# VectorE adds the scattered window sums to the node table from PSUM, with the mask as a per-partition scalar

## The chip, the cores and the metric

One core of one Trainium2 chip. The metric is the device time of one execution in microseconds, the median of several.

## The reference

Two layers of an equivariant graph network over 12,500 nodes and 200,000 edges, sorted by destination. Each layer gathers the source node's 32 features for every edge, computes from an MLP of the edge (64 hidden, 256 or 384 weights) the weights that mix them, and adds the resulting 32-wide message to the destination node. Around each layer stands a residual addition and a normalisation over the features.

```python
    edge_index = jnp.stack([src, dst])
    x = _layernorm(x + _L0_gnn_ref(x, edge_index, edge_attr_4, edge_attr_32, ...), axis=-1)
    x = _layernorm(x + _L1_gnn_ref(x, edge_weight, edge_attr_3, edge_index, ...), axis=-1)
```

In layer 0: `h = relu(edge_feat @ W1 + b1)`, `w = (h @ W2 + b2).reshape(e, 4, 8, 8)`, products of `w` with the gathered scalars and vectors and the edge's harmonics, and `segment_sum` over `dst`. Layer 1 has the same shape, with the distance as the MLP's input and seven paths.

## The kernel before

The edges are cut into 98 chunks of 2048 (16 tiles of 128). Each layer runs a loop over the chunks with two slots (z = 0, 1) for every buffer; the five engines each run their own program, ordered by semaphores alone. A prologue starts the first chunk, and a tail ends the last.

GpSimd gathers the source rows: 16 indirect DMAs per chunk, one per tile (`gather`, L340). It may run ahead by the two slots of `rows`.

TensorE computes the edge weights from the hidden values into PSUM (`weigh`, L624: 4 halves in layer 0, 8 in layer 1), adds up part of the products by a multiplication with the identity (`sum_products`, L637), and scatters the messages (`scatter`, L651): for each of 4 groups of 4 tiles it multiplies a one-hot matrix, made by ScalarE from the destination index modulo 128, with the messages cut into three bf16 parts, into `acc` (128 x 32 per group, in PSUM).

VectorE multiplies weights from PSUM with the gathered values (L899 and L906 in layer 0, L913 in layer 1; `multiply`), sums the rest of the products (L924), finishes the messages (L1022, L1026, L1029; L1072, L1078, L1086, L1095), cuts them (L932, L938), prepares the next chunk's rows (L948, L962, L974, L976; L952, L966, L983), and adds the previous chunk's windows to the node table (L990).

The window: the destinations of a group lie within 128 successive nodes, so they touch two neighbouring blocks of the table (2 x 32 columns). Which partition belongs to which block is said by two masks of 0 and 1 per group, kept in `plan` (16 columns of negative keys, then 4 x 2 masks). ScalarE's `split_windows` (L488) makes two masked copies of each group's `acc` in SBUF (`split`, 4 x 64 columns), 8 activations per chunk; VectorE's `add_window` (L990) adds 64 columns of `split` to the table at an address loaded into a register. The four windows of a chunk are added one after the other, because they may overlap; each waits for the one before. Other VectorE work stands between them.

In layer 0 the order in `body0` is: L948, window 0, window 1, L974, L976, window 2, L962, L1022, L1026, window 3, L1029, then the multiplications with the cuts L932 and L938 between them, and L924 twice. In layer 1 (`body1`): multiplications 0 to 5 between the message steps, L938, window 0, L966, window 1, L924, window 2, the seventh multiplication (L913), window 3, the eighth, L983, L924.

ScalarE: copies the chunk's plan (L450), computes the distances to an iota (L460), the one-hots (L469), the hidden values (L404, L406, L411), row copies (L434, L437, L438, L445), the copy of the sums (L478) and the masked copies (L488).

Of the kernel before, what the change touches and what calls it, by code (L numbers as in the profile page):

```python
# [9 lines left out]
ALU = mybir.AluOpType  # L10
# [68 lines left out]
BODY_STEPS, PROLOGUE_STEPS, TAIL_STEPS = (9, 10), (6, 7), (10, 12)  # L79


def build(nc, x, x_nodes, x_self, src, dst, dst_rows, sh, feat, rel, dist, identity, w1_0, b1_0, w2_0, si, w1_1, b1_1,
# [6 lines left out]
    with ExitStack() as ctx:  # L89
# [55 lines left out]
        plan_sb = slots(lambda z: sb(f"slot_plan{z}", [P, PLAN]))  # L145
# [4 lines left out]
        split = slots(lambda z: sb(f"split{z}", [P, GROUPS, 2 * FEAT]))  # L150
# [40 lines left out]
        class LayerSemaphores:  # L191


            def __init__(self, n):
# [28 lines left out]
                self.windows_split = ring("windows_split")  # L223
# [148 lines left out]
        def _(act):  # L372
# [90 lines left out]
            def one_hots(n, z, steps):  # L463

                s = layers[n]
                for half in range(2):
# [26 lines left out]
            def loop(n, count):  # L493
                s = layers[n]

                def body(i, z, r, last, steps):
# [10 lines left out]
                    if not tail:  # L507
                        distances(n, z1, r1, 1, steps)
                        if n == 0:
                            one_hots(n, z1, steps)  # L510
# [4 lines left out]
                    if n == 1:  # L515
                        if not tail:
                            one_hots(n, z1, steps)
                        if not last:
                            copy_rows(n, i + 1, z, r + 1)
                    if n == 0:  # L520
                        split_windows(n, z, r)
                        if not last:
                            hide(n, z, r + 1, 1)
# [4 lines left out]
                    if n == 1:  # L528
                        split_windows(n, z, r)

                with act.Fori(0, count) as j:
# [15 lines left out]
                    one_hots(n, 0, steps)  # L547
# [36 lines left out]
        def _(pe):  # L584
# [56 lines left out]
            def scatter(n, z, r):  # L641
# [4 lines left out]
                pe.wait_ge(s.windows_split[z], r)  # L646
# [644 lines left out]
```

## Time and profile before

| | us |
|---|---|
| runs | 4531.0, 4531.57, 4543.85 |
| median | 4531.57 |
| the profiled execution | 4544.37 |
| its span | 4542.6 |
| mean granted TensorE clock over the span | 0.922 of 2.4 GHz |

| engine | busy us | share |
|---|---|---|
| TensorE matmul | 3766.9 | 83% |
| VectorE | 3963.2 | 87% |
| ScalarE | 2346.9 | 52% |
| GpSimd | 3167.3 | 70% |

Layer 0 lies in about the first half of the span, layer 1 in the second. Times in the rows are from the start of the span; PE is TensorE, DVE VectorE, ACT ScalarE, POOL GpSimd. An instruction's row gives its duration; successive instructions of one engine overlap by a little, so that the next can start before the one in front has ended.

### The profile page before, as it was taken

What the parts mean: (1) busy time and instruction counts of PE and PEld (TensorE: products, weight loads), DVE (VectorE), ACT (ScalarE), POOL (GpSimd) and SP (SyncE); (2) the same over time, 40 slices, a digit from 0 to 9 for tenths busy, and PEclk for the clock granted to TensorE, in tenths of its full rate; (3) what the DMA queues carried; (4) which work ended last, traced back from release to release, by engine and by line L of the source; (5) the groups of instructions that cost most, each with busy time, mean ns of one, the idle gap of its engine ahead of it and who ended that gap; (6) DMA issues with size and microseconds to landing.
All of it is one profiled execution on the core that took longest, in us unless ns stands there. A gap on an engine that the chain in (4) does not pass through costs nothing.

```text
span 4542.6 us, 66084 instructions
## 1 busy us (share of the span) xinstructions
PE 3766.9 (83%) x19258; PEld 2237.4 (49%) x19258; DVE 3963.2 (87%) x4658; ACT 2346.9 (52%) x6473; POOL 3167.3 (70%) x3145
## 2 busy tenths in 40 slices
PE   5887887888787878887189999999999999999995
PEld 3555555555555555555034444444444444444442
DVE  6878788787887788877889999999999999999998
ACT  2555555555555555555045555555555555555553
POOL 6777777777777777777266667766766777667661
PEclk7998898888888988888589999999999999999997
DMA  2111111111111111111322121212121212121221
GB/s 91 28 23 28 28 23 28 28 23 28 27 25 28 23 28 28 23 28 23 76 49 43 34 43 34 43 34 44 34 43 34 43 34 43 34 43 37 40 40 21
DMA packets 206517, 159.45 MB, mean 35 GB/s; under 512 B 123073, under 2 KB 186562, under 8 KB 199234
## 3 DMA queue, kind: packets, MB, share of 16 engines
q1 hardware_dynamic: 76978, 89.79, 8.4%
q0 software_dynamic: 100352, 51.58, 7.9%
q10 hardware_dynamic: 29170, 17.88, 1.4%
q8 instruction: 7, 0.11, 0.0%
q14 instruction: 10, 0.08, 0.0%
HBM read 148.58 MB, written 10.43 MB: 35 GB/s over the span
## 4 chain that ended last, share of the span: by engine, by line
POOL 35%; PE 31%; issue 22%; DVE 10%; DVEq 1%; POOLq 0%; DMA 0%; ACT 0%; SPq 0%; ACTq 0%
POOL rows L340 35%; PE wps L624 16%; PE red L637 15%; DVE prod L913 6%; DVE t_b L1086 1%; DVE sums L924 0%; DVE q L983 0%; DVE t_b L842 0%; DVE work L823 0%; DVEq L897 0%; POOLq L357 0%; DVEq L1151 0%; DVE work L1195 0%; DVE table L1193 0%; DVE node_a L1196 0%
## 5 line engine op out<-in xcount | busy, mean ns | idle before, releaser
L624 PE MATMUL wps<-w_sb,hidden 128*128 128x256 f32 (+1 forms) x6272 | 2185.5, 506 | 669.6 <-DVE prod L906 394.8
L340 POOL DMA_INDIRECT rows<-x_rows,src x1568 | 1544.1, 985 | 755.7 <-issue 468.5
L624 PEld LDWEIGHTS wps<-w_sb,hidden 128*128 128x128 f32 x6272 | 1305.1, 213 | 1489.4 <-issue 518.5
L340 POOL DMA_INDIRECT rows<-in_x,src x1568 | 1615.2, 1030 | 506.3 <-issue 499.4
L637 PE MATMUL red<-prod,ident 128*128 128x384 f32 (+1 forms) x3136 | 1200.5, 536 | 0.0
L924 DVE TENSOR_REDUCE sums<-prod 128x192 f32<-128x1536 f32 (+2 forms) x392 | 1099.2, 2823 | 0.0
L460 ACT ACTIVATE gap<-iota,slot_plan 128x128 bf16<-128x128 f32 x3136 | 956.6, 387 | 264.1 <-DVE t_b L1086 179.4
L913 DVE TENSOR_TENSOR prod<-wps,q 128x896 f32<-128x896 f32 x784 | 844.8, 1086 | 96.3 <-PE wps L624 95.4
L637 PEld LDWEIGHTS red<-prod,ident 128*128 128x128 f32 x3136 | 594.8, 190 | 584.3 <-issue 396.5
L488 ACT ACTIVATE split<-acc,slot_plan 128x32 f32<-128x32 f32 x1568 | 300.1, 302 | 664.6 <-PE acc L651 635.2
L899 DVE TENSOR_TENSOR prod<-wps,q 128x768 f32<-128x768 f32 x392 | 374.0, 954 | 126.6 <-PE wps L624 126.2
L469 ACT ACTIVATE onehot<-gap 128x1024 bf16<-128x1024 bf16 x392 | 389.5, 1041 | 0.0
L906 DVE TENSOR_TENSOR prod<-wps,q 128x768 f32<-128x768 f32 x392 | 372.3, 950 | 0.0
L404 ACT ACTIVATE hidden<-hps,b_sb 64x512 f32<-64x512 f32 x196 | 134.9, 688 | 414.7 <-PE hps L603 414.7
L478 ACT ACTIVATE sums<-red 128x384 f32<-128x384 f32 (+1 forms) x196 | 105.9, 540 | 467.0 <-PE red L637 467.0
L948 DVE TENSOR_TENSOR t_a<-rows,geo 128x384 f32<-128x384 f32 x98 | 55.3, 564 | 289.3 <-DMA rows<-in_x,src 289.3
L651 PEld LDWEIGHTS acc<-msg,onehot 128*128 128x128 bf16 x3136 | 243.3, 96 | 81.9 <-issue 81.9
L651 PE MATMUL acc<-msg,onehot 128*128 128x32 bf16 x3136 | 255.8, 176 | 16.5 <-issue 15.4
L411 ACT ACTIVATE hidden<-mlp,b_sb,w1c_sb 64x1024 f32<-64x1024 f32 x196 | 231.0, 1226 | 72.2 <-issue 72.2
L651 PEld LDWEIGHTS acc<-rest,onehot 128*128 128x128 bf16 x3136 | 240.0, 96 | 43.1 <-issue 42.4
L651 PE MATMUL acc<-rest,onehot 128*128 128x32 bf16 x3136 | 255.3, 176 | 0.0
L651 PE MATMUL acc<-last_part,onehot 128*128 128x32 bf16 x3136 | 255.2, 176 | 0.0
(112 smaller groups left out, 2372.6 us busy)
## 6 DMA issues: line engine op xcount, KB each, us to landing
mlp<-in_dist SPq DMA_DIRECT2D x98, 512.0 KB, 5.0
mlp<-in_feat SPq DMA_DIRECT2D x98, 256.0 KB, 2.9
rows<-in_x,src POOLq DMA_INDIRECT x1568, 2.4
rows<-x_rows,src POOLq DMA_INDIRECT x1568
frames<-prod ACTq DMA_DIRECT2D x4, 1764.0 KB, 5.9
geo<-frames ACTq DMA_DIRECT2D x98, 72.0 KB, 1.9
src<-in_src SPq DMA_DIRECT2D x196, 8.0 KB, 1.6
geo<-in_sh ACTq DMA_DIRECT2D x98, 32.0 KB, 1.8
```

The lines of the kernel that those rows point to most:

```text
L340: nc.gpsimd.indirect_dma_start(out=rows[z][:, t, :], out_offset=None, in_=table_rows, in_offset=bass.IndirectOffsetOnAxis(ap=src_sb[z][:, ...
L411: nc.scalar.activation(hidden[0:HID, z, c0:c0 + 2 * SET], mlp_sb[z][0:HID, c0:c0 + 2 * SET], ACT.Relu, bias=b1_sb[0:HID, 1:2], scale=w1c_s ...
L460: ins = nc.scalar.activation(gap[:, t, :], iota[:], ACT.Abs, bias=plan_sb[z][:, t:t + 1])
L469: ins = nc.scalar.activation(onehot[z][:, t0:t1, :], gap[:, t0:t1, :], ACT.Relu, scale=-1.0, bias=1.0)
L488: ins = nc.scalar.activation(split[z][:, g, w * FEAT:(w + 1) * FEAT], acc[z][:, g * FEAT:(g + 1) * FEAT], ACT.Identity, scale=plan_sb[z][: ...
L624: ins = nc.tensor.matmul(wps[:, col:col + W_PATHS[n] * MM], hidden[:, z, e0:e0 + P], w2, start=True, stop=True)
L637: ins = nc.tensor.matmul(red[:, 0:cols], ident[:], pr[:, i, :, a:b, :], start=(i == 0), stop=(i == MUL - 1))
L651: ins = nc.tensor.matmul(acc[z][:, g * FEAT:(g + 1) * FEAT], onehot[z][:, t, :], cut[part][:, t, :], start=(tg == 0 and part == 0), stop=( ...
L899: nc.vector.tensor_tensor(pr[:, :, 1, t0:t0 + T, :].rearrange("p i t (m o) -> p t m i o", m=3), w[:, :, 3 * MM:4 * MM].rearrange("p t (i o ...
L906: ins = nc.vector.tensor_tensor(pr[:, :, 0, t0:t0 + T, :].rearrange("p i t (a o) -> p t a i o", a=3), w[:, :, 0:3 * MM].rearrange("p t (a ...
L913: ins = nc.vector.tensor_tensor(pr[:, :, 0, t0:t0 + T, :].rearrange("p i t (a o) -> p t a i o", a=7), w[:, :, 0:C].rearrange("p t (a i o) ...
L924: st.done(nc.vector.tensor_reduce(sums_by_half(n)[:, :, t0:t1, :], products(n)[:, :, :, t0:t1, :].rearrange("p i h t c -> p h t c i"), AX_ ...
```

## The change

`split` and `split_windows` go. VectorE's `add_window` reads `acc` in PSUM itself: for each group two scalar_tensor_tensor instructions of 32 columns, table = acc x mask + table, with the mask column as the per-partition scalar. The masks get a buffer of their own, `mask_sb`, apart from the keys in `plan_sb`, filled by a new ScalarE copy at the end of each body (`copy_masks`), which waits until VectorE has added the windows that used that slot before (`windows_added`) and signals `masks_copied`. `add_window` for the first group waits for `scattered` and `masks_copied`; after the last group it waits for its own last instruction and increments `windows_added`, for which TensorE's `scatter` waits in place of `windows_split`. ScalarE's `copy_plan` now waits for the one-hots of the slot, and `one_hots` for the scatter that read them. The first addition, which in the kernel before added a zeroed `split`, now reads a zeroed `acc` with zeroed masks. (In the prologue two steps are counted in place of one.)

```diff
-BODY_STEPS, PROLOGUE_STEPS, TAIL_STEPS = (9, 10), (6, 7), (10, 12)
+BODY_STEPS, PROLOGUE_STEPS, TAIL_STEPS = (9, 10), (7, 8), (10, 12)
...
-                act.wait_ge(layers[n].windows_split[z], r)
-                steps.done(nc.scalar.activation(plan_sb[z][:], plan[:, bass.ds(k, 1), :].rearrange("p k c -> p (k c)"),
-                                                ACT.Copy))
+                act.wait_ge(layers[n].onehot_ready[z], r)
+                steps.done(nc.scalar.activation(plan_sb[z][:], plan[:, bass.ds(k, 1), 0:TILES].rearrange(
+                    "p k c -> p (k c)"), ACT.Copy))
+
+            def copy_masks(n, k, z, r):
+
+                act.wait_ge(layers[n].windows_added[z], r)
+                nc.scalar.activation(mask_sb[z][:], plan[:, bass.ds(k, 1), TILES:PLAN].rearrange("p k c -> p (k c)"),
+                                     ACT.Copy).then_inc(layers[n].masks_copied[z], 1)
...
+                act.wait_ge(s.scattered[z], r)
...
-            def split_windows(n, z, r):
-
-                s = layers[n]
-                act.wait_ge(s.scattered[z], r + 1)
-                for g in range(GROUPS):
-                    for w in range(2):
-                        ins = nc.scalar.activation(split[z][:, g, w * FEAT:(w + 1) * FEAT],
-                                                   acc[z][:, g * FEAT:(g + 1) * FEAT], ACT.Identity,
-                                                   scale=plan_sb[z][:, TILES + g * 2 + w:TILES + g * 2 + w + 1])
-                ins.then_inc(s.windows_split[z], 1)
...
-                pe.wait_ge(s.windows_split[z], r)
+                pe.wait_ge(s.windows_added[z], r)
...
-            def add_window(g, cols, z, st):
-
+            def add_window(n, g, cols, z, r, st, final=False):
+
+                s = layers[n]
                 if g:
                     st.need(add_window.last)
+                else:
+                    dve.wait_ge(s.scattered[z], r)
+                    dve.wait_ge(s.masks_copied[z], r)
                 window = flat[:, bass.ds(cols[g], 2 * FEAT)]
-                add_window.last = st.done(nc.vector.tensor_tensor(window, window, split[z][:, g, :], ALU.add))
+                for w in range(2):
+                    part = window[:, w * FEAT:(w + 1) * FEAT]
+                    ins = nc.vector.scalar_tensor_tensor(
+                        out=part, in0=acc[z][:, g * FEAT:(g + 1) * FEAT],
+                        scalar=mask_sb[z][:, g * 2 + w:g * 2 + w + 1], in1=part, op0=ALU.mult, op1=ALU.add)
+                add_window.last = st.done(ins)
+                if g == GROUPS - 1 and not final:
+                    st.need(add_window.last)
+                    dve.sem_inc(s.windows_added[z], 1)
...
-                dve.wait_ge(s.windows_split[z1], r + z)
-                add_window(0, cols, z1, st)
-                add_window(1, cols, z1, st)
+                add_window(0, 0, cols, z1, r + z, st)
+                add_window(0, 1, cols, z1, r + z, st)
...
-                    st.need(st.done(nc.vector.memset(split[1][:], 0.0)))
+                    st.done(nc.vector.memset(mask_sb[1][:], 0.0))
+                    st.need(st.done(nc.vector.memset(acc[1][:, 0:GROUPS * FEAT], 0.0)))
```

In ScalarE's body the masked copies stood before the second half of the hidden values in layer 0 and at the end in layer 1; `copy_masks` stands at the end in both.

## Rows read from the trace of the kernel before

**Rows 1.** The page: busy time, share of the span and instructions of each engine.

```profile
PE 3766.9 (83%) x19258; PEld 2237.4 (49%) x19258; DVE 3963.2 (87%) x4658; ACT 2346.9 (52%) x6473; POOL 3167.3 (70%) x3145
```

**Rows 2.** Busy times by stretch: one chunk of layer 0, one of layer 1.

```profile
core 0: us, PE busy (x) PEld busy (x) DVE busy (x) ACT busy (x) POOL busy (x), PEclk, DMA share, GB/s
1005.93:1027.33 21.40, 16.84 (x100) 11.81 (x99) 17.26 (x23) 11.81 (x33) 16.46 (x16) 0.92 0.10 14
3297.43:3319.82 22.39, 20.52 (x97) 10.21 (x96) 21.69 (x24) 12.11 (x34) 16.07 (x18) 1.00 0.33 63
```

**Rows 3.** Timeline of GpSimd in layer 0: start us, duration us, instruction, idle before.

```profile
1003.51 0.94 POOL L340 DMA_INDIRECT rows<-in_x,src  x1 [0.30 <-issue]
1004.76 0.94 POOL L340 DMA_INDIRECT rows<-in_x,src  x1 [0.30 <-issue]
1006.01 1.30 POOL L340 DMA_INDIRECT rows<-in_x,src  x1 [0.30 <-issue]
1007.61 0.95 POOL L340 DMA_INDIRECT rows<-in_x,src  x1 [0.30 <-issue]
1008.87 1.64 POOL L340 DMA_INDIRECT rows<-in_x,src  x1 [0.30 <-issue]
1010.81 0.94 POOL L340 DMA_INDIRECT rows<-in_x,src  x1 [0.30 <-issue]
...
1013.31 1.25 POOL L340 DMA_INDIRECT rows<-in_x,src  x1 [0.30 <-issue]
```

**Rows 4.** Timeline of VectorE over the same stretch of layer 0.

```profile
1005.93 0.56 DVE L948 TENSOR_TENSOR t_a<-rows,geo 128x384 f32<-128x384 f32 x1 [3.62 <-DMA rows<-in_x,src]
1006.41 0.58 DVE L990 TENSOR_TENSOR table<-table,split 128x64 f32 x2
...
1007.10 0.67 DVE L976 TENSOR_TENSOR q<-rows,geo 128x384 f32<-128x384 f32 x1
...
1008.28 0.55 DVE L1022 TENSOR_TENSOR t_b<-sums,geo 128x384 f32<-128x384 f32 x1
1008.74 0.29 DVE L1026 TENSOR_TENSOR msg<-sums 128x128 f32<-128x128 f32 x1
1008.94 0.22 DVE L990 TENSOR_TENSOR table<-table,split 128x64 f32 x1
1009.08 0.60 DVE L1029 TENSOR_TENSOR msg<-t_b,sums 128x384 f32<-128x384 f32 x1
...
1010.46 0.95 DVE L906 TENSOR_TENSOR prod<-wps,q 128x768 f32<-128x768 f32 x1
...
1013.05 0.69 DVE L932 TENSOR_TENSOR rest<-msg 128x512 f32<-128x512 f32 x1
```

**Rows 5.** Costliest groups: busy us, mean ns of one, idle before. Layer 0's gathers.

```profile
L340 POOL DMA_INDIRECT rows<-in_x,src x1568 | 1615.2, 1030 | 506.3 <-issue 499.4
```

**Rows 6.** Timeline of VectorE in layer 1, around the four windows of a chunk.

```profile
3297.43 0.21 DVE L990 TENSOR_TENSOR table<-table,split 128x64 f32 x1
3297.57 1.34 DVE L966 TENSOR_REDUCE q<-t_a 128x384 f32<-128x1152 f32 x1
...
3301.35 0.21 DVE L990 TENSOR_TENSOR table<-table,split 128x64 f32 x1
3301.78 1.09 DVE L913 TENSOR_TENSOR prod<-wps,q 128x896 f32<-128x896 f32 x1 [0.22 <-PE wps L624]
3302.79 0.21 DVE L990 TENSOR_TENSOR table<-table,split 128x64 f32 x1
3303.29 1.09 DVE L913 TENSOR_TENSOR prod<-wps,q 128x896 f32<-128x896 f32 x1 [0.28 <-PE wps L624]
```

**Rows 7.** Timeline of TensorE in layer 1, ahead of the sums L637.

```profile
3314.10 1.77 PE L624 MATMUL wps<-w_sb,hidden 128*128 128x448 f32 x4 [0.51 <-DVE prod L913]
```

**Rows 8.** Costliest groups: ScalarE's masked copies and the old window addition.

```profile
L990 DVE TENSOR_TENSOR table<-table,split 128x64 f32 x792 | 172.3, 218 | 23.6 <-ACT split L488 4.8 <-issue 4.2
...
L488 ACT ACTIVATE split<-acc,slot_plan 128x32 f32<-128x32 f32 x1568 | 300.1, 302 | 664.6 <-PE acc L651 635.2
```

**Rows 9.** Groups of instructions by form: L773, in the set-up.

```profile
L773 DVE SCALAR_TENSOR_TENSOR table<-wps,table 128x512 f32<-128x512 f32 x6 | 3.9, 686 | 1.4 <-PE wps L592 1.4
L773 DVE SCALAR_TENSOR_TENSOR table<-wps,table 128x64 f32<-128x64 f32 x1 | 0.2, 216 | 0.0
```

More of the change, by code:

```diff
@@ L144, in build @@
         hidden = sb("hidden", [P, RING, CHUNK])
-        plan_sb = slots(lambda z: sb(f"slot_plan{z}", [P, PLAN]))
+        plan_sb = slots(lambda z: sb(f"slot_plan{z}", [P, TILES]))
+        mask_sb = slots(lambda z: sb(f"slot_masks{z}", [P, 2 * GROUPS]))
         gap = sb("gap", [P, TILES, P], BF16)
@@ L222, in __init__ @@
                 self.scattered = ring("scattered")
-                self.windows_split = ring("windows_split")
+                self.windows_added = slots(lambda z: sem(f"l{n}_windows_added{z}"))
+                self.per_chunk.append((self.windows_added[0], 1))
+                self.masks_copied = ring("masks_copied")
                 self.dve_body = sem(f"l{n}_dve_body")
@@ L461, in distances, with one_hots @@
                 steps.done(ins)
-            def one_hots(n, z, steps):
+            def one_hots(n, z, r, steps):
                 s = layers[n]
+                act.wait_ge(s.scattered[z], r)
                 for half in range(2):
@@ L509, in body @@
                         if n == 0:
-                            one_hots(n, z1, steps)
+                            one_hots(n, z1, r1, steps)
                     if not last:
@@ L516, in body @@
                         if not tail:
-                            one_hots(n, z1, steps)
+                            one_hots(n, z1, r1, steps)
                         if not last:
                             copy_rows(n, i + 1, z, r + 1)
[L520 to L523, printed above, removed]
+                    if n == 0 and not last:
+                        hide(n, z, r + 1, 1)
                     if n == 1 and not last:
@@ L527, in body @@
                         copy_sums(n, z1, r1)
-                    if n == 1:
-                        split_windows(n, z, r)
+                    copy_masks(n, k, z, r)
                 with act.Fori(0, count) as j:
@@ L546, in loop @@
                         distances(n, 0, r0, half, steps)
-                    one_hots(n, 0, steps)
+                    one_hots(n, 0, r0, steps)
                     if n == 1:
@@ L1026, in body0 @@
                 nc.vector.tensor_tensor(msg[z][:, :, 0:MUL], sm[:, :, 0, :], sm[:, :, 1, :], ALU.add)
[L1027 removed]
+                add_window(0, 3, cols, z1, r + z, st)
                 dve.wait_ge(s.geo_used[z], r + 1)
@@ L1103, in body1 @@
                 cols = load_columns(k)
-                dve.wait_ge(s.windows_split[z1], r + z)
-                add_window(0, cols, z1, st)
+                add_window(1, 0, cols, z1, r + z, st)
                 if not last:
@@ L1108, in body1 @@
                     project_sum(1, z)
-                add_window(1, cols, z1, st)
+                add_window(1, 1, cols, z1, r + z, st)
                 if not tail:
                     sum_tiles(1, z1, r1, 0, st)
-                add_window(2, cols, z1, st)
+                add_window(1, 2, cols, z1, r + z, st)
                 if not tail:
                     multiply(1, z1, r1, 6)
-                add_window(3, cols, z1, st)
+                add_window(1, 3, cols, z1, r + z, st)
                 if not tail:
```

7 lines of the change are left out of this document (2 added, 5 removed).

## The prediction

> **What bounds the kernel now.** I read the page's busy shares first. No engine is idle enough to be ruled out, since VectorE has 87%, TensorE 83% and GpSimd 70% [rows 1], but these are means over two layers with different limits, so I read each layer from one chunk of its own. In layer 0 a chunk takes 21.40 us, of which VectorE is busy for 17.26 us; in layer 1 it takes 22.39 us, of which VectorE is busy for 21.69 and TensorE for 20.52 [rows 2].
>
> Layer 0 is set by GpSimd. Its 16 gather instructions for a chunk follow each other without a break: undisturbed, one starts 1.25 us after the other, of which 0.94 us is the instruction [rows 3]. Sixteen times 1.25 is 20.0 us of the 21.4. VectorE stood idle for 3.62 us before it could start the body of this chunk, and what it waited for was the gathered rows [rows 4]. The missing 1.4 us are in the gathers that take longer: 1.30, 1.64 and 1.25 us in place of 0.94 [rows 3], together 1.37 us. Over the layer the mean is 1030 ns [rows 5], so with 0.945 for an undisturbed one 1568 x (1.030 - 0.945) = 133 us, or 1.36 us a chunk.
>
> What lengthens them is seen by laying GpSimd's rows on VectorE's. The gather at 1006.01 ends its extra 0.36 us when L948 is nearly through (1005.93 + 0.56 = 1006.49). The gather at 1008.87 starts inside an unbroken run L1022, L1026, L990, L1029, ending at 1009.68; its extra 0.70 us brings it to 1009.57. The gather at 1013.31 meets L932, ending at 1013.74, and gets 0.31 us, to 1013.62 [rows 3, 4]. In all three the gather is held until about 0.12 us before the end of the VectorE instruction that runs when it starts, or of the last in an unbroken run, and all these instructions read two tensors from SBUF. The gather at 1010.81, which starts in L906 with one input in PSUM and one in SBUF, takes 0.94 us. The one at 1007.61 starts 0.16 us before the end of L976 and takes 0.95 us though an L990 follows: a gather that finds a gap gets through [rows 3, 4].
>
> The Trainium skill says the same of the mechanism (GPSIMD Engine Reference, "Key points": GpSimd's SBUF interfaces are shared with VectorE, with contention from VectorE instructions with two SBUF inputs). It speaks for this change: the added instruction has one input in PSUM.
>
> Layer 1 is set by a loop between VectorE and TensorE. VectorE waits for weights 0.22 us before the seventh L913 of the chunk and 0.28 us before the eighth [rows 6]; TensorE in turn has waited 0.51 us for an L913 [rows 7] and then does the last quarters of the weights with the 16 matmuls of L637 between them. So up to those two L913, TensorE's chain is the later one and VectorE has a little slack.
>
> **The change part by part.** ScalarE loses 8 copies per chunk of 302 ns (L488) and gets one of eight mask columns, an instruction of the same kind. It stood waiting for TensorE's scatter before those copies, 635 us in all [rows 8]; it is late nowhere. I cost this at nothing; what hides it is ScalarE's own idle time, and without that it would be a gain. The waits that ask for scattered sums, for the free one-hot and for the free mask are on work a whole body earlier; they are met, also at nothing. TensorE's scatter now waits for VectorE's addition of two chunks before, also long done.
>
> VectorE has, per chunk, 8 scalar_tensor_tensor (PSUM and SBUF in, 32 wide) in place of 4 tensor_tensor (64 wide). The old one takes 218 ns [rows 8], and the next instruction starts 0.14 us after it (3297.43 to 3297.57, [rows 6]). The new form stands in L773: 216 ns for 64 and 686 ns for 512 columns [rows 9], so 1.05 ns a column and 182 ns for 32. With the same overlap of 0.08 us the next starts 0.10 us later. A window costs 0.20 in place of 0.14: +0.06 to 0.08. If each pair ran without any overlap and with a semaphore's gap (two L990 in a row span 0.58 us, which is 0.14 us between them [rows 4]), it would be 8 x 0.32 - 4 x 0.14 = 2.0 us a chunk. I take the overlapped cost, since neighbours on VectorE overlap everywhere in [rows 4, 6] and the two halves of a window do not wait for each other.
>
> The Trainium skill prices a VectorE instruction with a PSUM source at 120 cycles plus columns against 58 (VectorE: DVE Perf Modes, "The TRN2 errata"). By that estimate the eight would cost 8 x 158 - 4 x 127 ns = 0.76 us a chunk more, not 0.3; the L773 rows do not bear out the difference.
>
> Besides, the first window has one more wait (masks) and every second half its own address step, which I take as +0.1 us at the first window only, the others standing behind long instructions. The fourth window ends with a wait for its own end and a semaphore increment: last half starts at +0.10, ends at +0.28, then 0.14 of semaphore gap and some 0.07 for the increment, so the next instruction starts at 0.49 in place of 0.14: +0.35 us. Queued behind it are L1029 in layer 0 and the eighth L913 in layer 1.
>
> Layer 1: extra before the seventh L913 is 3 x 0.07 + 0.1 = 0.31 us; the slack there is 3301.78 - (3301.35 + 0.14) = 0.29. Extra before the eighth is 0.35; slack 3303.29 - (3302.79 + 0.14) = 0.36 [rows 6]. Nearly all is hidden under TensorE; 0.04 us a chunk is left, 98 x 0.04 = +4 us. The cover is thin: together 0.65 us of extra are free, and each 0.1 us beyond them costs 9.8 us.
>
> Layer 0: L974 and L976 move by about 0.13 us, L1022 and L1026 by 0.2, L1029 and all behind it by 0.55, and VectorE still has 3.62 - 0.55 us before the rows land. The gathers, counted from L948's start, are at 0.08 (held 0.36 as now), 1.68 (meets L976, now ending at 1.97: held 0.17), 3.09 (meets L1026, held 0.08, and then finds the PSUM instructions where L990 closed the run), 4.42, 5.67, 6.91 and 8.16, where L932 now ends at 8.36 with its last 0.12 free: held 0.0 to 0.1. The sum is about 0.65 us in place of 1.37, or 98 x 0.72 = -71 us. If instead the gathers met VectorE at random, a run of length R (less its last 0.12) would hold R x R / 2.5 us a chunk: now L974 and L976 0.87 us, L1022 to L1029 1.28 us and L932 and L938 0.56 each give 0.30 + 0.66 + 0.13 + 0.13; after, the long run splits into 0.64 and 0.48, giving 0.16 + 0.09 in place of 0.66: 0.41 us, -40 us. The phase is not random, since a chunk's start is set by the last gather, so I lean to the walk, but its last step lies on an edge: -60 us.
>
> Sum: -60 + 4 = -56 us. The profiled execution took 4544.4 us, of which 4542.6 are its span, so it would take 4488. It is the slowest of those shown; the median is 4531.57, and from it the time is 4476 us.
>
> **Rivals.** (A) The holds only move. The gathers, coming earlier, meet L932 or L938, which are as long as before; layer 0 gives 10 to 30 us. For it: every body step after the fourth window shifts by half a microsecond, a good part of the gathers' pitch. Against it: the 0.70 us hold needs the run that the change breaks. Time: about 4511 us.
>
> (B) VectorE becomes the late one in layer 1. The place is the stretch from the first window to the eighth L913, where 0.65 us is free. At the upper cost of 2.0 us a chunk the overrun is 1.3 us, +130 us, less 60 in layer 0: 4602 us. It decides from an extra of 0.65 + 60/98 = 1.3 us a chunk on. For it: 97% busy in that layer; two short dependent instructions with a gap stand in [rows 4]. Against: the overlap of all neighbours. At 0.76 us a chunk for the eight, the overrun would be 0.67 - 0.29 + 0.48 - 0.36 = 0.50 us and the result 4521 us; that is what the Trainium skill's estimate above comes to.
>
> (C) The new instruction holds the gathers as the old did (it still reads the table in SBUF, and the mask as a scalar), so nothing is gained in layer 0 and little lost in layer 1: 4531 to 4545 us. Against: L906, with PSUM and SBUF in, holds none [rows 3, 4].
>
> **How the numbers follow.** Forecast 0.58, A 0.17, C with a mild B 0.13, B 0.12. The forecast's own range, from -80 to -30 us, is 4452 to 4502. The range for 8 in 10 takes in A and the near end of C: 4450 to 4540. A measurement can tell about 0.3% (14 us) from no change. Faster by more: the forecast and most of A, 0.73. Within: C and the rest of A, 0.14. Slower: B and a part of C, 0.13.
>
> **What would show it.** Right: the mean of the layer 0 gather falls from 1030 ns to about 985 to 1000, the 1.64 us gathers are gone, VectorE still idles before L948's successor for over 1.5 us, and a layer 0 chunk takes 20.6 to 20.9 us; scalar_tensor_tensor at about 180 ns; a layer 1 chunk at 22.4 us, with less or no waiting before the last two L913. Wrong: VectorE without a wait before the eighth L913 and a layer 1 chunk above 22.6 us (B), gathers of 1.2 us and more behind L932 and L938 (A), or gathers held while the new instruction runs (C).

## The result

The changed kernel takes 4573.51 us (4561.79 to 4586.49, six runs) against 4532.73 us for the kernel before: a ratio of 1.0084, 95% interval 1.0064 to 1.0105. It is slower by just under 1% (38 to 41 us) where 56 us less were forecast. Its profiled execution has a span of 4571.9 us, that of before 4542.6: 29 us more.

In the changed file the lines are shifted. L991 is the new window addition (before: L990), L458 the copy of the masks, L342 the gather (L340), L908 layer 1's multiplication (L913), L919 the reductions (L924), L943 the first step of a layer 0 body (L948), L619 and L632 TensorE's weights and sums (L624 and L637), L646 the scatter (L651).

Of the page of the changed kernel, the busy shares and the costliest groups (busy us, mean ns of one, idle before and what ended it), against [rows 1, 5, 8]:

```profile
PE 3816.5 (83%) x19258; PEld 2234.8 (49%) x19258; DVE 4109.7 (90%) x5452; ACT 2066.2 (45%) x5101; POOL 3077.5 (67%) x3145
...
L342 POOL DMA_INDIRECT rows<-in_x,src x1568 | 1542.0, 983 | 543.7 <-issue 481.0
...
L991 DVE SCALAR_TENSOR_TENSOR table<-acc,slot_masks,table 128x32 f32 x1584 | 320.3, 244 | 171.9 <-ACT slot_masks L458 149.8
```

Three things are to be seen. The gathers of layer 0 are shorter, 983 ns in place of 1030, as forecast. The new instruction takes 244 ns and not 182. And VectorE now stands idle 149.8 us before it, for ScalarE's copy of the masks, a wait that the forecast had priced at nothing.

The layers go apart. The stretches run from the first to the last message cut (L938 before, L933 after) of each layer, which is 97 chunks; the columns are those of [rows 2]. First the kernel before, then the changed one:

```profile
91.69:2175.74 2084.06, 1679.69 (x9664) 1189.84 (x9662) 1669.36 (x2222) 1135.19 (x3177) 1569.16 (x1528) 0.90 0.13 26
2324.92:4505.38 2180.47, 2008.80 (x9281) 997.99 (x9279) 2088.84 (x2222) 1162.47 (x3177) 1485.48 (x1510) 0.98 0.20 38
```

```profile
91.75:2154.01 2062.26, 1688.41 (x9668) 1195.17 (x9667) 1747.58 (x2610) 1008.60 (x2500) 1496.02 (x1527) 0.90 0.13 26
2301.01:4532.49 2231.48, 2050.32 (x9281) 990.88 (x9279) 2153.57 (x2610) 1012.71 (x2499) 1470.36 (x1511) 0.98 0.19 37
```

Layer 0 gains 22 us (21.49 to 21.26 us a chunk in the mean), layer 1 loses 51 us (22.48 to 23.00). From cut to cut the median chunk of layer 1 went from 22.32 to 22.72 us, which is 39 us of the 51. The rest is in chunks in which TensorE's granted clock fell to half for a while (1.2 in place of 2.4 GHz). There are 23 chunks of 24.2 us in the changed kernel and none after them makes anything up. The kernel before has 21 of 23.7 us, and 18 of them are followed by a chunk of 21.9 us. Two rows of the kernel before, a chunk at full clock and the next with a share at half:

```profile
2553.12:2575.44 22.32, 20.50 (x98) 1.00 0.09 14
2575.44:2599.10 23.66, 22.28 (x99) 0.93 0.32 60
```

**Layer 1, around the windows.** VectorE's timeline in the changed kernel, the same place as [rows 6]:

```profile
3310.70 0.68 DVE L933 TENSOR_TENSOR last_part<-rest 128x512 bf16<-128x512 f32 x1
3311.34 0.41 DVE L991 SCALAR_TENSOR_TENSOR table<-acc,slot_masks,table 128x32 f32 x2
3311.67 1.34 DVE L961 TENSOR_REDUCE q<-t_a 128x384 f32<-128x1152 f32 x1
...
3315.62 0.41 DVE L991 SCALAR_TENSOR_TENSOR table<-acc,slot_masks,table 128x32 f32 x2
3315.94 1.08 DVE L908 TENSOR_TENSOR prod<-wps,q 128x896 f32<-128x896 f32 x1
3316.94 0.41 DVE L991 SCALAR_TENSOR_TENSOR table<-acc,slot_masks,table 128x32 f32 x2
3317.57 1.09 DVE L908 TENSOR_TENSOR prod<-wps,q 128x896 f32<-128x896 f32 x1 [0.23 <-DVE table L991]
```

A window (two instructions, x2) holds the next instruction off by 0.32 us (3315.62 to 3315.94) where it was 0.14. The seventh multiplication no longer waits for TensorE, and the eighth starts 0.63 us after the fourth window and waits, not for TensorE, but for VectorE's own last instruction. All of the 0.65 us of cover, the time VectorE could lose behind TensorE at no cost, is used up.

**Layer 0, start of a body.** VectorE, and ScalarE over the same stretch:

```profile
1016.60 0.54 DVE L943 TENSOR_TENSOR t_a<-rows,geo 128x384 f32<-128x384 f32 x1
1018.46 0.95 DVE L991 SCALAR_TENSOR_TENSOR table<-acc,slot_masks,table 128x32 f32 x4 [1.32 <-ACT slot_masks L458]
```

```profile
1017.50 0.49 ACT L487 ACTIVATE sums<-red 128x384 f32<-128x384 f32 x1 [3.78 <-PE red L632]
1018.02 0.21 ACT L458 ACTIVATE slot_masks<-plan 128x8 f32 x1
```

The wait for the rows (3.62 us in [rows 4]) is gone, since the gathers are ahead. In its place stands a wait for the mask copy. That copy needs nothing of this chunk, but on ScalarE it is queued behind the copy of TensorE's sums, which ends at 1017.99. VectorE's first window now follows TensorE's last sums, and the body has become a loop of VectorE, TensorE and ScalarE.

### The profile page after: what moved, and what is told of

It reads as the page before. It is cut to its first block, busy times and chain, and to the rows that moved or that the text cites. A ratio compares the mean times of both kernels' runs of the same rounds, so it can differ in the third digit from the quotient of the medians.

```text
span 4571.9 us, 66982 instructions
## 1 busy us (share of the span) xinstructions
PE 3816.5 (83%) x19258; PEld 2234.8 (49%) x19258; DVE 4109.7 (90%) x5452; ACT 2066.2 (45%) x5101; POOL 3077.5 (67%) x3145
## 4 chain that ended last, share of the span: by engine, by line
PE 33%; issue 29%; DVE 28%; DVEq 5%; ACT 3%; POOL 1%; ACTq 0%; DMA 0%; SPq 0%; POOLq 0%
PE wps L619 18%; PE red L632 11%; DVE prod L908 8%; DVE table L991 5%; PE hps L598 4%; DVE msg L1101 3%; DVEq L1001 3%; DVE prod L901 2%; ACT hidden L408 1%; DVE rest L927 1%; DVE t_b L1028 1%; DVE t_b L1092 1%; DVEq L991 1%; ACT hidden L406 1%; POOL rows L342 1%
## 5 line engine op out<-in xcount | busy, mean ns | idle before, releaser
L619 PE MATMUL wps<-w_sb,hidden 128*128 128x256 f32 (+1 forms) x6272 | 2233.0, 511 | 648.1 <-DVE prod L901 364.9
L342 POOL DMA_INDIRECT rows<-x_rows,src x1568 | 1527.6, 974 | 830.9 <-issue 475.5
L619 PEld LDWEIGHTS wps<-w_sb,hidden 128*128 128x128 f32 x6272 | 1302.4, 214 | 1518.1 <-issue 522.1
L342 POOL DMA_INDIRECT rows<-in_x,src x1568 | 1542.0, 983 | 543.7 <-issue 481.0
L632 PE MATMUL red<-prod,ident 128*128 128x384 f32 (+1 forms) x3136 | 1200.3, 536 | 0.0
L919 DVE TENSOR_REDUCE sums<-prod 128x192 f32<-128x1536 f32 (+2 forms) x392 | 1098.3, 2820 | 0.0
L908 DVE TENSOR_TENSOR prod<-wps,q 128x896 f32<-128x896 f32 x784 | 841.9, 1083 | 81.2 <-PE wps L619 57.9
L632 PEld LDWEIGHTS red<-prod,ident 128*128 128x128 f32 x3136 | 595.5, 190 | 583.5 <-issue 399.8
L991 DVE SCALAR_TENSOR_TENSOR table<-acc,slot_masks,table 128x32 f32 x1584 | 320.3, 244 | 171.9 <-ACT slot_masks L458 149.8
L646 PEld LDWEIGHTS acc<-msg,onehot 128*128 128x128 bf16 x3136 | 243.2, 96 | 84.1 <-issue 84.1
L646 PE MATMUL acc<-msg,onehot 128*128 128x32 bf16 x3136 | 255.8, 176 | 16.6 <-issue 16.6
L646 PEld LDWEIGHTS acc<-rest,onehot 128*128 128x128 bf16 x3136 | 239.9, 96 | 42.9 <-issue 42.8
L646 PE MATMUL acc<-rest,onehot 128*128 128x32 bf16 x3136 | 255.2, 176 | 0.0
L646 PE MATMUL acc<-last_part,onehot 128*128 128x32 bf16 x3136 | 255.2, 176 | 0.0
L646 PEld LDWEIGHTS acc<-last_part,onehot 128*128 128x128 bf16 x3136 | 239.4, 96 | 0.0
```

Of the source, the lines that this page charges most:

```text
L342: nc.gpsimd.indirect_dma_start(out=rows[z][:, t, :], out_offset=None, in_=table_rows, in_offset=bass.IndirectOffsetOnAxis(ap=src_sb[z][:, ...
L619: ins = nc.tensor.matmul(wps[:, col:col + W_PATHS[n] * MM], hidden[:, z, e0:e0 + P], w2, start=True, stop=True)
L632: ins = nc.tensor.matmul(red[:, 0:cols], ident[:], pr[:, i, :, a:b, :], start=(i == 0), stop=(i == MUL - 1))
L646: ins = nc.tensor.matmul(acc[z][:, g * FEAT:(g + 1) * FEAT], onehot[z][:, t, :], cut[part][:, t, :], start=(tg == 0 and part == 0), stop=( ...
L908: ins = nc.vector.tensor_tensor(pr[:, :, 0, t0:t0 + T, :].rearrange("p i t (a o) -> p t a i o", a=7), w[:, :, 0:C].rearrange("p t (a i o) ...
L919: st.done(nc.vector.tensor_reduce(sums_by_half(n)[:, :, t0:t1, :], products(n)[:, :, :, t0:t1, :].rearrange("p i h t c -> p h t c i"), AX_ ...
```

## The experiments

Some kernels ran several times, since the chips fell in two groups. On three chips the kernel before took 4518 to 4533 us, as in the result. On three others it took 6937 to 7026 us. In the traces from those (l0_only, l0_only_early_b, inc_late_c) the 48 short matmuls of a chunk's scatter are spread over 1.35 to 17 us, about 5 in the median, where they take 1.35 in the traces of before and after; whether that is all of the difference no run shows. Each ratio is to the kernel before on the same chip; in what follows "the 4530 chips" and "the 6970 chips" name the groups.

**The changed kernel again** (4530 chip), and on the same chip the kernel before with a third of the scatter's matmuls:

> The changed kernel as it is, on these chips. Theory 1 (in layer 0 VectorE's first window waits for a mask copy behind the sums, so any delay of TensorE's sums is passed on to the next chunk): much slower than before here, about 7350 us like inc_late_l1, with VectorE waiting over 10 us a chunk for the masks in layer 0. Rival (the loss is VectorE's own work, 0.4 to 0.5 us a chunk in layer 1, whatever TensorE does): within 60 us of the kernel before.

> The kernel before with one of the three bf16 parts of the messages scattered, 16 matmuls a chunk in place of 48 (the two small remainders of the message are left out of the sums; VectorE's cuts and all waits stay). On the chips of these runs the kernel before takes 6960 to 7000 us, and the traces show TensorE's 48 scatter matmuls spread over 4 to 14 us in place of 1.35. Theory 1 (TensorE is starved of instructions in the long train of short ones, and all else is as on the first chip): with a third of them the time falls to 4500 to 4700 us, and edits can be compared again in the state of the traces of before and after. Rival (these chips are slower in something else, such as TensorE's clock): above 6300 us.

```diff
-                    for part in range(3):
+                    for part in range(1):
...
```

The changed kernel took 4574.25 us against 4527.41: ratio 1.0109, 1.0089 to 1.0130. The loss repeats, within 60 us of the kernel before, as the rival said. VectorE's waits in layer 0 were again 149.7 us for the mask copy. The question about the 6970 chips could not be answered here, for this chip was not one of them. The kernel with two of the three parts left out was slower, 4611.78 us (two runs), ratio 1.0187 (1.0166 to 1.0208). Its time lies in the range that its theory 1 gave, but on a 4530 chip that says nothing of the theory. Why it was slower is taken up in the last section.

**Layer 0 alone, masks late or early** (6970 chips):

> Layer 0 as in the changed kernel, layer 1 as in the kernel before. Theory 1 (the two layers add up: layer 0 gave back 0.22 us a chunk, 97 x 0.225 = 22 us, and layer 1 lost 97 x 0.526 = 51 us): about 4533 - 22 = 4511 us, layer 0 chunks at a mean of 21.26 us and layer 1 chunks at 22.48 us. Rival (the loss lies in what the layers share, such as the set-up or TensorE's clock, and stays with the new layer 0): above 4533 us, with layer 1 chunks at more than 22.7 us.

> The changed kernel with one move: in layer 0 ScalarE copies the masks where the masked copies stood, before the second half of the hidden values, and not after the copy of the sums. Theory 1 (VectorE's first window waited 1.56 us a chunk for the mask copy, which was queued behind the sums of the chunk, and this wait hides what the shorter gathers gave): the wait is gone, layer 0 is again set by the gathers at 16 x 1.25 + 0.6 = 20.6 us a chunk in place of 21.26, 97 x 0.66 = 64 us less than the changed kernel, about 4508 us. Rival (the wait is only where VectorE's time collects; TensorE's weights and sums are late anyway, and the wait moves to the next instruction that needs the sums): layer 0 chunks stay at 21.1 to 21.3 us and the time at 4565 to 4575 us.

> Layer 0 as changed and with the masks copied early, layer 1 as in the kernel before. Theory 1: both effects add, layer 0 at 20.6 us a chunk, that is 97 x (21.49 - 20.6) = 86 us below the kernel before, about 4447 us. Rival (layer 0 is not bound by the gathers once the mask copy is early): about 4511 us as with the masks late.

The move of the masks, in ScalarE's body:

```diff
+                    if n == 0:
+                        copy_masks(n, k, z, r)
                     if n == 0 and not last:
                         hide(n, z, r + 1, 1)
...
-                    copy_masks(n, k, z, r)
+                    if n == 1:
+                        copy_masks(n, k, z, r)
```

With late masks 7320.81 us (ratio 1.0487, 1.0458 to 1.0515), with early masks and both layers changed 6809.24 (0.9762), with early masks and layer 1 as before 6798.26 (0.9747). Repeated on two more of these chips, masks_early_b and masks_early_c gave 0.9800 and 0.9776, l0_only_early_b and l0_early_c 0.9747 and 0.9743. The expectations were written for a 4530 chip, which none of these repeats met:

> The same kernel as masks_early, since the first comparison ran on a chip where the kernel before took 6977 us and TensorE's work was far longer than in the traces of before and after. Theory 1 (VectorE's first window waits for a mask copy queued behind the copy of the sums; early, layer 0 is set by the gathers again): layer 0 chunks at 20.6 us, about 4508 us. Rival (the wait moves to the next instruction that needs the sums): layer 0 chunks at 21.1 to 21.3 us, 4565 to 4575 us.

> The same kernel as l0_only_early (layer 0 as changed with early masks, layer 1 as before). Theory 1: layer 0 at 20.6 us and layer 1 at 22.48 us a chunk, about 4447 us. Rival (layer 0 is not set by the gathers): about 4511 us.

> The changed kernel with the mask copy early in layer 0. Theory 1: layer 0 at 20.6 us in place of 21.26, layer 1 as in the changed kernel, about 4574 - 64 = 4510 us. Rival (the wait moves to the next instruction that needs the sums): layer 0 at 21.1 to 21.3 us, 4565 to 4575 us.

> Layer 0 as changed with the mask copy early, layer 1 as in the kernel before; the kernel before takes 4527 us again. Theory 1 (layer 0 set by the gathers once the mask copy is early, layer 1 untouched): layer 0 at 20.6 us and layer 1 at 22.48 us a chunk, about 4445 us. Rival (layer 0 is held by the loop of VectorE and TensorE, the mask wait is only where it shows): layer 0 at 21.2 us, about 4505 us.

No time that had been expected could be met on such a chip, but the ratios tell something: with layer 1 as before, the place of one small copy in ScalarE's queue is worth 7% (7320.81 to 6798.26 us). VectorE's longest waits on such a chip follow, inc_late_c (late masks, and a move in layer 1 that is described below) and then masks_early_c. The columns are us in total, times and longest; "remote" is a releaser that the profile can't name, L908 and L911 are layer 1's multiplication, L991 and L994 the window addition, and L1031 is layer 0's t_b step (L1022 before).

```profile
DVE table L991 <- ACT slot_masks L458: 1441.6, 96, 18.2
DVE prod L908 <- remote: 1292.4, 90, 25.9
```

```profile
DVE prod L911 <- remote: 1300.5, 93, 15.6
DVE table L994 <- issue: 896.8, 105, 11.7
DVE t_b L1031 <- ACT sums L487: 217.4, 91, 11.3
```

In l0_only and l0_only_early, which differ in the place of the copy alone, it is the same: 1488.4 us for the masks, against 889.6 before the window and 202.5 for the sums. Early, VectorE no longer waits for the masks. It waits for the sums where it needs them, further on in the body (217 us in masks_early_c); another 897 us stand before a window, for nothing that the profile shows. So the mask copy does couple each chunk to TensorE's sums. What that costs depends on how late the sums are.

**The same at 4530 us.** One of the repeats met a 4530 chip:

> Layer 0 as changed with the mask copy early, layer 1 as in the kernel before. If the kernel before takes about 4530 us here: theory 1 (layer 0 set by the gathers, layer 1 untouched) about 4445 us, layer 0 chunks at 20.6 us; rival (layer 0 held by VectorE and TensorE) about 4505 us, chunks at 21.2 us. If it takes about 6970 us: 6790 us as in the three comparisons before.

It took 4511.17 us against 4526.30: ratio 0.9967 (0.9955 to 0.9980). That is near the rival's number, 4505, and 66 us from mine. But its reason is not the rival's. VectorE's waits in layer 0 (in this file L966 is the first step of a body, L948 before; L917 a multiplication, L1064 the step after the fourth window, L1029 before, and L1020 the window addition):

```profile
DVE t_a L966 <- DMA rows<-in_x,src: 161.0, 96, 3.9
DVE prod L917 <- PE wps L642: 117.2, 103, 1.6
DVE msg L1064 <- DVE table L1020: 15.1, 96, 0.5
```

VectorE waits for the rows again, in every body, and GpSimd's gathers have 30% of the chain of work that ended last (35% before, 1% in the changed kernel). So layer 0 is set by the gathers, as theory 1 said. The gathers are not as short as it said. Over layer 0 their extra time is 1.07 us a chunk (0.62 in the changed kernel, where they do not matter, 1.36 before). GpSimd, and VectorE at the same place:

```profile
1014.37 1.27 POOL L346 DMA_INDIRECT rows<-in_x,src  x1 [0.30 <-issue]
1015.95 1.33 POOL L346 DMA_INDIRECT rows<-in_x,src  x1 [0.30 <-issue]
1017.58 1.17 POOL L346 DMA_INDIRECT rows<-in_x,src  x1 [0.30 <-issue]
```

```profile
1014.27 0.56 DVE L966 TENSOR_TENSOR t_a<-rows,geo 128x384 f32<-128x384 f32 x1 [1.37 <-DMA rows<-in_x,src]
1014.74 0.94 DVE L1020 SCALAR_TENSOR_TENSOR table<-acc,slot_masks,table 128x32 f32 x4
1015.60 0.28 DVE L992 TENSOR_TENSOR q<-rows,geo 128x128 f32<-128x128 f32 x1
1015.80 0.68 DVE L994 TENSOR_TENSOR q<-rows,geo 128x384 f32<-128x384 f32 x1
...
1017.63 0.29 DVE L1061 TENSOR_TENSOR msg<-sums 128x128 f32<-128x128 f32 x1
```

The gather at 1015.95 is held until 1016.34, L994 ending at 1016.48; the one at 1017.58 until 1017.81, L1061 ending at 1017.92. The 1.64 us gather is gone. In its place are two short holds, and two more behind the cuts L950 and L956 (gathers of 1.08 us at 1022.79 and 1.17 us at 1026.68).

The whole of layer 0 bears the reading out. Of its 1527 gathers 326 are held by more than 0.05 us in the kernel before, 233 of 1526 in the changed one and 412 in l0_early_d. Each of these holds ends 0.11 to 0.16 us before the end of a VectorE instruction with two SBUF inputs. None of the gathers that start while VectorE is idle, reduces or multiplies from PSUM is held (1100 before). And 51 gathers of the changed kernel start while the new window addition runs: none is held, so rival C of the prediction is out.

**The price of the mask as an operand.** no_mask_operand, with repeats no_mask_operand_b and no_mask_c, all on 6970 chips:

> The changed kernel with the number 1.0 in place of the mask column in the eight scalar_tensor_tensor of a chunk; the multiplication by the mask is left out, all waits and copies stay. Theory 1 (what the prediction had too small is the fixed cost of a scalar operand read from SBUF): the instruction takes 180 to 185 ns in place of 244, the next starts 0.10 us after it in place of 0.16, layer 1 gets back 8 x 0.06 us less what is hidden, 0.3 to 0.4 us a chunk, 30 to 40 us: 4535 to 4545 us. Rival (the 60 ns come from the PSUM operand at 32 columns or from the address register): still 235 to 250 ns and 4573 us.

> The same kernel as no_mask_operand: the number 1.0 in place of the mask column, so the multiplication by the mask is left out. There the instruction took less time or not independently of TensorE; on a chip like the first, theory 1 (a scalar operand read from SBUF costs 60 ns an instruction): 182 ns each, next start after 0.10 us, layer 1 at about 22.35 to 22.45 us in the median chunk, 4535 to 4545 us. Rival (the PSUM operand or the address step costs it): 235 to 250 ns, 4573 us.

> The changed kernel with the number 1.0 in place of the mask column (the multiplication by the mask is left out). Theory 1 (60 ns for a scalar operand read from SBUF): about 182 ns an instruction, the next start after 0.10 us, median layer 1 chunk 22.35 to 22.45 us, 4535 to 4545 us. Rival (the cost lies in the PSUM operand or the address step): 235 to 250 ns and 4574 us.

```diff
-                        scalar=mask_sb[z][:, g * 2 + w:g * 2 + w + 1], in1=part, op0=ALU.mult, op1=ALU.add)
+                        scalar=1.0, in1=part, op0=ALU.mult, op1=ALU.add)
```

Their times (7057.67, 7042.67 and 7077.85 us, ratios 1.0124 to 1.0144) can't be compared with the expected ones. The instruction's own duration is, as it has the same 244 ns on both groups of chips with the mask. The group of no_mask_c, and then a third window in its timeline with what follows:

```profile
L991 DVE SCALAR_TENSOR_TENSOR table<-acc,table 128x32 f32 x1584 | 237.4, 186 | 1299.3 <-ACT slot_masks L458 1271.1
```

```profile
5026.53 0.28 DVE L991 SCALAR_TENSOR_TENSOR table<-acc,table 128x32 f32 x2
5026.73 1.08 DVE L908 TENSOR_TENSOR prod<-wps,q 128x896 f32<-128x896 f32 x1
```

It takes 186 ns against 182 worked out from [rows 9], and a window of two takes 0.20 us of VectorE's time, as forecast. With the mask column they are 244 ns and 0.32. So the 60 ns are the scalar operand, and the PSUM operand costs nothing beyond what [rows 9] show. What the operand is worth in time on a 4530 chip was not measured. On the 6970 chip of no_mask_c layer 0 takes 3094 us from first to last cut, against 3345 us in inc_late_c, whose layer 0 is the same but for the mask: 2.6 us a chunk for 0.5 us of VectorE's time, and no run shows what multiplies it.

**The wait after the fourth window.** inc_late_l1 (7342.07 us, 1.0538), inc_late_c (7311.73, 1.0495), both on 6970 chips, and inc_late_d on a 4530 chip are the same kernel:

> The changed kernel with one move in layer 1: the wait for the fourth window's own end and the increment of windows_added stand after the eighth L908 and the difference, ahead of the last reduction, not right after the fourth window. Theory 1 (in layer 1 the overrun is made of 0.29 us from dearer windows before the seventh product and 0.50 us behind the fourth window, of which 0.32 is this wait): the eighth product starts 0.32 us after the fourth window in place of 0.64, the median layer 1 chunk falls from 22.72 to 22.40 us, the time by about 30 us to 4543 us. Rival (the dearer windows alone have made VectorE the late one, and the wait is repaid elsewhere in the body): 22.6 us or more a chunk, above 4560 us.

> The changed kernel with the increment of windows_added moved behind the eighth L908 and the difference in layer 1. Theory 1 (the overrun is 0.29 us before the seventh product and 0.50 behind the fourth window, 0.32 of it the wait): median layer 1 chunk 22.40 us in place of 22.72, about 4543 us. Rival (VectorE's dearer windows alone make it late): 22.6 us or more a chunk, above 4560 us.

> The changed kernel with the increment of windows_added moved behind the eighth L908 and the difference in layer 1; layer 0 as changed. If the kernel before takes about 4530 us: theory 1 (0.29 us of overrun before the seventh product, less the 0.36 us of cover before the eighth, plus 0.18 for the fourth window: about 0.1 us left) median layer 1 chunk 22.4 us in place of 22.72, 4574 - 30 = 4544 us. Rival (the dearer windows alone make VectorE late) 22.6 us or more, above 4560 us.

```diff
                 if not last:
                     differ(z, r + 1, st)
+                st.need(add_window.last)
+                dve.sem_inc(s.windows_added[z1], 1)
                 if not tail:
                     sum_tiles(1, z1, r1, 1, st)
```

(and no wait or increment after the fourth window in layer 1). On the 4530 chip it took 4512.30 us against 4527.70: ratio 0.9967, 0.9955 to 0.9980, 61 us below the changed kernel's 4573.51 on its chip (53 us by the two ratios), where 30 had been expected. The fourth window of a layer 1 chunk, and then the stretches of the two layers:

```profile
3318.44 0.40 DVE L991 SCALAR_TENSOR_TENSOR table<-acc,slot_masks,table 128x32 f32 x2
3318.76 1.08 DVE L908 TENSOR_TENSOR prod<-wps,q 128x896 f32<-128x896 f32 x1
```

```profile
91.56:2153.64 2062.08, 1687.57 (x9664) 1194.23 (x9662) 1747.82 (x2610) 1008.98 (x2500) 1494.93 (x1527) 0.90 0.12 26
2303.62:4470.58 2166.95, 1997.85 (x9281) 981.43 (x9279) 2145.33 (x2610) 1012.81 (x2499) 1463.51 (x1509) 1.00 0.19 38
```

The eighth multiplication starts 0.32 us after the window and not 0.63. The median chunk is 22.41 us, within 0.01 of what was expected, so the mechanism stands: 97 x 0.31 = 30 us of the 64.5 us by which this layer is shorter. The rest came with the clock: the granted clock of layer 1 is 1.00, none of the 23 chunks of 24.2 us is left (23 x 1.5 = 34 us), and layer 1 is shorter than in the kernel before (2167 against 2180 us) though its median chunk is longer.

**The moved operand alone** was to show that an input in PSUM, and no shift of VectorE's steps, takes the holds away:

> The kernel before with one operand moved: L990 adds 64 columns of an idle, zeroed part of acc's PSUM bank in place of the masked copies in SBUF, so the window sums are left out of the table; all waits, copies and the number of instructions stay. Theory 1 (a gather is held by runs of VectorE instructions with two SBUF inputs, and an input in PSUM breaks the run): the extra time of the layer 0 gathers falls from 1.36 us a chunk to 0.5 to 0.8 us, and L990 itself takes about 216 ns; where layer 0 is set by the gathers it loses 0.5 to 0.8 us a chunk. Rival (the shorter gathers of the changed kernel come only from VectorE's later steps having moved against them): 1.2 to 1.4 us a chunk as before.

```diff
-                add_window.last = st.done(nc.vector.tensor_tensor(window, window, split[z][:, g, :], ALU.add))
+                add_window.last = st.done(nc.vector.tensor_tensor(window, window, acc[z][:, 256:256 + 2 * FEAT], ALU.add))
...
```

(Those 64 columns are set to zero once, and the window sums are left out of the table.)

It ran on a 6970 chip only: 7039.88 us, ratio 1.0056. The instruction took 216 ns as expected, and the gathers' extra time was 0.21 us a chunk, but there they stand idle for other reasons (974.8 us for ScalarE's row copy), and the kernel before has no trace on such a chip to compare with. So it is inconclusive, and the claim that PSUM breaks the run rests on the traces of layer 0. L1061, L1020 and L1064 of l0_early_d stand as L1026, L990 and L1029 did. In the kernel before 89 gathers that meet this place are held through the window to the end of L1029; in l0_early_d 94 are held to the end of L1061, and none to that of L1064.

**Both moves** (4530 chip):

> The changed kernel with both moves: the mask copy early in layer 0, the increment late in layer 1. If the kernel before takes about 4530 us here: theory 1 (the two layers add up: layer 0 as in l0_early_d, 2055 us from first to last cut, layer 1 as in inc_late_d, 2167 us) about 4505 us. Rival (layer 1's full clock in inc_late_d came by chance, and 19 chunks of it fall to half clock for 1.4 us each): about 4530 us.

4501.54 us (4498.32 to 4504.66) against 4524.84: ratio 0.9947, 0.9934 to 0.9961. It is the fastest kernel of the study, 0.5% below the kernel before with an interval clear of 1. Its stretches add up from the two single moves, 2055 and 2167 us:

```profile
92.54:2146.48 2053.94, 1667.75 (x9668) 1179.59 (x9667) 1745.95 (x2610) 1018.09 (x2500) 1538.03 (x1527) 0.90 0.12 26
2296.52:4463.44 2166.92, 1998.05 (x9281) 981.48 (x9279) 2145.36 (x2610) 1012.77 (x2499) 1469.89 (x1509) 1.00 0.19 38
```

## Why the prediction was wrong, step by step

The forecast was -60 us in layer 0 and +4 in layer 1. The profiles show -22 and +51, so both terms of the sum failed, layer 1's by 47 us and layer 0's by 38.

**What bounds each layer** held. Layer 0 was set by the gathers: as soon as the mask wait is out of the way VectorE waits for rows again. The prediction called the cover in layer 1 thin at 0.65 us and priced each 0.1 us beyond it at 9.8 us. The extra is about 1.1 us: 0.04 ahead of the first window (0.64 us from L933 to it, 0.60 before), 0.54 in three windows and 0.49 behind the fourth. The overrun is 0.4 us, and the median chunk grew by 0.40 us.

**The step that failed first** is "The new form stands in L773: 216 ns for 64 and 686 ns for 512 columns [rows 9], so 1.05 ns a column and 182 ns for 32." The rows of L773 have the number SI_SCALE as their scalar; the new instruction has a column in SBUF. The form was taken for the same and was not. no_mask_operand and its repeats show 185 to 186 ns for the form priced, the traces of the changed kernel 244 for the one that was added. Per window that is 0.18 us extra in place of 0.07, so 0.54 and not 0.21 before the seventh multiplication.

The Trainium skill's estimate of 0.76 us a chunk for the eight (VectorE: DVE Perf Modes, "The TRN2 errata") was set aside in the prediction. The measured extra is 8 x 0.16 - 4 x 0.14 = 0.72 us. The sum is nearly right, but not for the reason the page gives, a dearer PSUM source. Without the mask operand the extra is 8 x 0.10 - 4 x 0.14 = 0.24 us, and in window_from_idle_psum the old L990 takes 216 ns with an input in PSUM against 218 with both in SBUF.

**The wait behind the fourth window** was priced rightly in kind and a little low, +0.35 us; it is 0.63 - 0.14 = 0.49, of which 0.12 is again the operand. The text had even said that nearly all of it fits under 0.36 us of cover. Both terms were added up against a margin of hundredths. The windows were off by 0.54 - 0.21 = 0.33 us and this term by 0.14. The 12 us of layer 1 that the median does not hold are the falls of the clock, a term that the sum did not have.

**The step on ScalarE** failed in another way: "the waits that ask ... for the free mask are on work a whole body earlier; they are met, also at nothing." True of what the mask copy waits for, false of where it stands. It is issued at the end of ScalarE's body, behind the copy of the sums, and VectorE's first window waits for it. That wait the prediction put at +0.1 us. It counted the instructions that the mask copy needs and not those queued ahead of it on its engine. The wait took 1.56 us a chunk (149.8 us / 96) and came in the place of the wait for rows. Its net price on a 4530 chip is small, since with it the mean chunk is 21.26 us and without it 21.17 us: layer 0 of both_moves, 2053.9 us, against 2062.1 of inc_late_d. On a 6970 chip it is over 500 us (l0_only against l0_only_early).

**The gathers** went as rival A said: the holds moved. The fall of the extra time to 0.62 us a chunk in the changed kernel looks like the forecast 0.65, but it is that of a kernel whose VectorE is held elsewhere. Where the gathers set the pace it is 1.07 us (l0_early_d, mean of a gather 1012 ns). The walk through the phases started from VectorE's steps after the windows, and these were misplaced by the dearer windows: L976's successor was put to end at 1.97 us after the body's start and ends at 2.21, which holds the next gather for 0.39 us in place of 0.17. The walk gave 0.72 us less a chunk and the random-phase estimate 0.41; 0.29 was measured. That the measured 983 ns of the changed kernel meet the forecast's sign of being right is luck.

**Rival B** is what happened in layer 1, at about half the price that its upper bound gave, and it was said to decide from 1.3 us of extra on. That point moved, for it had been set against a gain of 60 us in layer 0; with 22 us it lies at 0.65 + 22/97 = 0.88 us. An extra of 1.1 us is beyond it. The range ended at 4540 us and left out the slower side, although B's bounds reached there and stood at 0.12.

## What to carry to other kernels

Price an instruction from a row of the same operand kinds, the scalar's included: here a column in place of a number cost 60 ns in each of eight instructions a chunk, and a wait for the engine's own last result cost 0.3 us a chunk until it was moved to a later place. A new small copy inherits the waits of everything ahead of it in its engine's queue; place it before the instruction that waits for the slow engine. Where the engine that sets the pace is held by another at certain moments, a shift of a few tenths of a microsecond can move the holds rather than remove them. Here the estimate from the mean (0.41 us) came nearer to the measured 0.29 than the walk through the phases (0.72).

## What the runs showed that had not been expected

TensorE's granted clock changed with edits that give it no more work. In layer 1, leaving out its last few us, the kernel before spends 72 us at half clock, in 21 spells, and the changed one 80 us, in 24 (after_again: 15 spells). With the increment moved there is none, in the traces of two kernels, and the mean clock of the span is 0.931 to 0.933 in all their 11 runs, against 0.921 to 0.927 in those of the changed kernel. TensorE's instructions are the same (9281 in each stretch; 2009 us busy of 2180 before, 1998 of 2167 after the move). The kernel with a third of the scatter's matmuls does the opposite, in layer 1:

```profile
2307.71:4569.59 2261.88, 2028.79 (x6177) 965.06 (x6175) 2085.23 (x2223) 1162.45 (x3177) 1496.07 (x1511) 0.94 0.18 36
```

Less work for TensorE, a clock of 0.94 in place of 0.98, and a median chunk of 23.67 us. It lost 81 us in layer 1.

What these kernels differ in is TensorE's longest idle time of a chunk. It lies behind the scatter, where the next weights wait for a multiplication on VectorE. The row of it in the kernel before, the changed one, inc_late_d and the one with a third of the scatter:

```profile
3308.81 4.78 PE L624 MATMUL wps<-w_sb,hidden 128*128 128x448 f32 x12 [1.36 <-DVE prod L913]
```

```profile
3300.36 4.78 PE L619 MATMUL wps<-w_sb,hidden 128*128 128x448 f32 x12 [1.41 <-DVE prod L908]
```

```profile
3301.88 4.78 PE L619 MATMUL wps<-w_sb,hidden 128*128 128x448 f32 x12 [1.24 <-DVE prod L908]
```

```profile
3304.83 4.78 PE L624 MATMUL wps<-w_sb,hidden 128*128 128x448 f32 x12 [2.08 <-DVE prod L913]
```

The medians of its 96 occurrences in layer 1 are 1.36, 1.41, 1.23 and 2.12 us, and the clock fell 21, 24, 0 and 80 times. In the first two every fall came within 1 us after the end of such an idle time, in the last within 1.5 us of it. So the fall goes with that idle time, and a shorter scatter makes it longer. No run changed the idle time alone, so that it is the cause is likely and not shown. The effect, 20 to 80 us, is as large as the change that was to be judged.

And the same program took 4530 us on some chips and 6970 on others. In a row of inc_late_c a scatter matmul of 0.18 us comes after 1.17 us of idle time with nothing that the profile shows it waited for:

```profile
5007.65 0.18 PE L646 MATMUL acc<-last_part,onehot 128*128 128x32 bf16 x1 [1.17 <-issue]
```

The cause stays open.
